# Scores of a self-attention pair as two 64-row plain fp32 products, in place of stacked and split q and k

## The reference, cut to what matters

```
DIM, HEADS, DHEAD = 160, 20, 64
q = (norm(x) @ wq1), k = (norm(x) @ wk1), v = (norm(x) @ wv1)      # 160 -> 20 heads x 64
scores = einsum('bhnd,bhmd->bhnm', q, k) * DHEAD ** -0.5           # 4 x 20 x 512 x 512
attn = softmax(scores); out = einsum('bhnm,bhmd->bhnd', attn, v)
x = out @ wo1 + bo1 + x
```

## Time and profile before

| | |
|---|---|
| median of 3 runs (lowest, highest) | 1209.48 us (1207.38, 1214.39) |
| span of the profiled execution, first to last instruction | 1209.3 us |
| mean granted TensorE clock of that execution, as a share of full | 0.983 |
| busy: TensorE / VectorE / ScalarE / GpSimd | 1143.5 / 748.8 / 621.4 / 355.7 us |
| self-attention, from its first q projection to its last output projection | 213 to 888 us of the span |
| bytes moved by the stacking DMAs' queue in all | 75.54 MB |

### The profile page before, as it was taken

The page is one execution under the profiler, slowest core; times in us unless marked ns, Lnnn a source line. Parts: engine busy times, 40 slices in busy tenths (PEclk is TensorE's granted clock), DMA queues, the critical chain, the costliest instruction groups (busy, mean ns, idle before and its releaser), DMA issues. The chain is left out here.

```text
span 1209.3 us, 21134 instructions
## 1 busy us (share of the span) xinstructions
PE 1143.5 (95%) x6348; PEld 766.6 (63%) x6348; DVE 748.8 (62%) x1758; ACT 621.4 (51%) x1370; POOL 355.7 (29%) x470
## 2 busy tenths in 40 slices
PE   7999999599999899999999999999989999999898
PEld 3555555456666666657566567666577778786787
DVE  4374574377777377774777775777637575757253
ACT  2543444356566366663565663656516464646242
POOL 2330321233433133432334332333213131312110
PEclk9999999799999999999999999999989999999899
DMA  6500000444444244444244443445120000000000
GB/s 167 114 1 1 0 1 1 104 105 105 106 105 105 56 105 106 111 99 107 58 111 107 95 108 81 111 103 118 42 55 2 1 0 0 0 1 1 1 22 22
DMA packets 43427, 76.69 MB, mean 63 GB/s; under 512 B 13316, under 2 KB 21444, under 8 KB 43332
## 3 DMA queue, kind: packets, MB, share of 16 engines
q1 hardware_dynamic: 43332, 75.54, 27.0%
HBM read 11.29 MB, written 1.31 MB: 10 GB/s over the span
## 5 line engine op out<-in xcount | busy, mean ns | idle before, releaser
L524 ACT ACTIVATE sa_probs<-banks,sa_negmax 128x512 f32<-128x512 f32 x320 | 220.9, 690 | 268.1 <-DVE sa_negmax L595 267.5
L665 POOL TENSOR_SCALAR sa_probs<-sa_probs,sa_inverse 128x512 f32<-128x512 f32 x320 | 223.1, 698 | 418.6 <-DVE sa_inverse L600 418.6
L595 DVE TENSOR_REDUCE sa_negmax<-banks 128x1 f32<-128x512 f32 x320 | 219.5, 686 | 104.8 <-PE banks L417 104.6
L427 PEld LDWEIGHTS banks<-ident,sa_probs 128*128 128x128 f32 x1280 | 146.5, 140 | 150.1 <-issue 69.1
L605 DVE COPY sa_turned<-banks 128x512 f32<-128x512 f32 x240 | 162.8, 679 | 66.4 <-PE banks L427 66.0
L427 PE MATMUL banks<-ident,sa_probs 128*128 128x128 f32 x1280 | 200.1, 279 | 1.1 <-issue 1.1
L446 PE MATMUL banks<-sa_turned,sa_v 128*64 128x512 f32 x640 | 172.6, 617 | 3.0 <-ACT sa_turned L535 1.7
L416 PE MATMUL banks<-sa_k_stack,sa_q_stack 128*128 128x512 f32 x320 | 144.8, 453 | 19.3 <-DMA sa_k_stack<-sa_k_parts 8.2
L417 PE MATMUL banks<-sa_k_stack,sa_q_stack 128*128 128x512 f32 x320 | 127.8, 399 | 0.0
L1537 POOL TENSOR_TENSOR ca_probs<-ca_probs,ca_inverse 128x616 f32<-128x616 f32 x40 | 48.8, 1219 | 162.4 <-DVE ca_inverse L1485 162.4
L416 PEld LDWEIGHTS banks<-sa_k_stack,sa_q_stack 128*128 128x128 f32 x320 | 61.3, 192 | 28.8 <-ACT sa_probs L524 13.6
(11 more groups left out here) (189 smaller groups left out, 1992.2 us busy)
## 6 DMA issues: line engine op xcount, KB each, us to landing
sa_k_stack<-sa_k_parts SPq DMA_DIRECT2D x160, 256.0 KB, 4.2
sa_q_stack<-sa_q_parts SPq DMA_DIRECT2D x160, 128.0 KB, 2.3
w_o<-in_L_xattn_wo SPq DMA_DIRECT2D x2, 800.0 KB, 6.3
out<-x SPq DMA_DIRECT2D x4, 320.0 KB, 2.5
x<-in_x SPq DMA_DIRECT2D x1, 960.0 KB, 5.3
ad_raw_main<-in_L_xattn_wq SPq DMA_DIRECT2D x1, 640.0 KB, 4.6
ad_raw_main<-in_L_xattn_wk SPq DMA_DIRECT2D x1, 640.0 KB, 7.4
ad_raw_main<-in_L_xattn_wv SPq DMA_DIRECT2D x1, 640.0 KB, 10.0
```

The source lines that it names most:

```text
L427: last = pe.transpose(b_turn[n % 2][:, q * P:(q + 1) * P], probs[:, h % PS, q, k * P:(k + 1) * P], ident[:])
L524: act.activation(probs[:, h % PS, q, :], b_scores[n % 2], ACT.Exp, bias=negmax[:, c:c + 1], accum_out=total[:, c:c + 1]).then_inc(s_exp.se ...
L595: dve.tensor_reduce(negmax[:, c:c + 1], b_scores[n % 2], AX_X, ALU.max, negate=True).then_inc(s_max.sem, 1)
L665: pool.tensor_scalar(probs[:, h % PS, q, :], probs[:, h % PS, q, :], inverse[:, c:c + 1], 1.0, ALU.mult, ALU.mult).then_inc(s_norm.sem, 1)
```

## The change

- Scores: `q_all` and `k_all` hold a pair's q and k unsplit, head 0 on partitions 0 to 63, head 1 on 64 to 127, as the projection leaves them. `scores(b, u)` multiplies both heads of the pair for one query block, one head on array rows 0 to 63 and one on rows 64 to 127, each as one plain fp32 product (L368 in the changed file), into two banks of their own.
- The rounding of q and k, the remainders and all eight DMAs per pair are gone. ScalarE copies q, VectorE copies k.
- The order of work is in units. One maximum (VectorE) of 128 x 2 x 512, two exponentials, one reciprocal, two scalings and eight transposes make up one unit. Turned tiles for head 1 are copied by ScalarE in every second unit, the others by VectorE.
- PSUM: scores take four banks instead of two; `b_out` and `b_proj` become one bank each instead of two. So projections of q, k and v each wait for the copy of the one before, and the output projection uses the turned tiles' banks.
- After every unit with `u % 4` of 0, 1 or 2, the q, k or v of pair `u // 4 + 2` is projected; after `u % 4 == 3` none is. The normalised x is turned in two halves, at units 23 and 27, into the one projection bank. Before `pv` of the last unit, the output projection's products of the first eight pairs for the first 128 rows are made (four pairs before).

**TensorE, middle of a pass, a stretch without a projection, before**: turning head 0, scores of one block (`sa_k_stack`, `sa_q_stack`), `pv` for both heads, turning head 1.

The diff, cut to its core:

```diff
-    LEAD, LAG = 10, 2
-    NB = H1 * QT
-    PAIRB = 2 * QT
+    NU = NPAIR * QT
+    LEAD = 5
...
-    LN_AT = 37
-    TURN_AT = (NPAIR - 3) * PAIRB + 1
-    PROJECT, ROUND, REST = (20, 19, 16), (19, 18, 15), (18, 17)
-    START = {1: (1, 0), 2: (1, 1), 3: (1, 2), 8: (2, 0), 9: (2, 1)}
+    RING = 8
+    LN_AT = 12
+    TURN_MAIN, TURN_TAIL, ROUND_AT = 23, 27, 31
+    START = {0: (1, 0), 1: (1, 1), 2: (1, 2)}
+    def part_at(u):
+        j, what = u // QT + 2, u % QT
+        return (j, what) if what < 3 else None
...
-        q_stack = sb("q_stack", [P, 2, 2, S], F32R)
-        k_stack = sb("k_stack", [P, 2, 2, 2, S], F32R)
-        q_parts = sb("q_parts", [P, 2, S], F32R)
-        k_parts = sb("k_parts", [P, 2, S], F32R)
+        q_all = sb("q_all", [P, 2, S])
+        k_all = sb("k_all", [P, 2, S])
...
-        b_scores, b_turn, b_out, b_proj = banks[0:2], banks[2:4], banks[4:6], banks[6:8]
+        b_scores, b_turn, b_out, b_proj = [banks.pair(0), banks.pair(2)], banks[4:6], banks[6], banks[7]
...
-                for e, rows, half, to in places:
-                    sp.dma_start(k_stack[to, s, e, :, :].bitcast(F32), k_parts[rows, :, :].bitcast(F32)).then_inc(s_stack[s].sem, 16)
...
+            def scores(b, u):
+                j, q = divmod(u, QT)
+                if q == 0:
+                    pe.wait_ge(s_ksb.sem, s_ksb.at(b, j))
+                pe.wait_ge(s_exp.sem, s_exp.at(b, 2 * u - 3))
+                bank = b_scores[u % 2]
+                for e in range(2):
+                    rows = slice(e * HD, (e + 1) * HD)
+                    last = pe.matmul(bank[:, e, :], q_all[rows, j % 2, q * P:(q + 1) * P], k_all[rows, j % 2, :], start=True, stop=True)
+                last.then_inc(s_scores.sem, 1)
...
+            def batch(b, more):
+                for u in range(NU):
+                    m = u + LEAD
+                    if m < NU:
+                        scores(b, m)
+                    elif more:
+                        scores(b + 1, m - NU)
+                    if u >= 1:
+                        pv(b, u - 1)
+                    turns(b, u)
...
+                wait_turned_copied(pe, b, NU - 1, 0)
+                pe.wait_ge(s_att.sem, s_att.at(b, NPAIR - 2))
+                project_out(0, 0, NPAIR - 2)
+                pv(b, NU - 1)
...
+            def exps(b, u):
+                j, q = divmod(u, QT)
+                act.wait_ge(s_max.sem, s_max.at(b, u))
+                if q == 0:
+                    act.wait_ge(s_turn.sem, s_turn.at(b, 2 * QT * (j - 1) - 1))
+                for e in range(2):
+                    act.activation(probs[:, j % 2, e, q, :], b_scores[u % 2][:, e, :], ACT.Exp, bias=negmax[:, u % RING, e:e + 1],
+                                   accum_out=total[:, u % RING, e:e + 1]).then_inc(s_exp.sem, 1)
...
-                dve.tensor_reduce(negmax[:, c:c + 1], b_scores[n % 2], AX_X, ALU.max, negate=True).then_inc(s_max.sem, 1)
+                dve.tensor_reduce(negmax[:, u % RING, :], b_scores[u % 2], AX_X, ALU.max, negate=True).then_inc(s_max.sem, 1)
```

More of the change, by code:

```diff
@@ L611, in update @@
                         dve.wait_ge(s_bias.sem, s_bias.at(b, 0))
[L612 to L623 removed]
+                    xt = x[:, bass.ds(b * QT + 2 * half, 2), :].rearrange("p a d -> p (a d)")
@@ L625, in batch @@
+                    dve.tensor_tensor(xt, b_turn[half][:, 0:2 * D], xt, ALU.add).then_inc(s_x.sem, 1)
+            copy_k(0, 0)
+            for u in range(LEAD):
+                maxima(0, u)
+                if u in START and START[u][1] == 1:
+                    copy_k(0, START[u][0])
+                if u >= 1:
+                    inverses(0, u - 1)
             def batch(b, more):
-                for n in range(NB):
-                    m = n + LEAD
-                    if m < NB:
+                for u in range(NU):
+                    m = u + LEAD
+                    if m < NU:
```

411 lines of the change are left out of this document (167 added, 244 removed).

## The result

The changed kernel takes 1244.23 us (median of 4 runs, 1241.88 to 1246.55), the kernel before 1208.84 us beside it. The ratio is 1.0286, with a 95% interval of 1.0237 to 1.0335: slower by 2.9%. The forecast was 1236 us with a range of 1216 to 1267. The profiled execution has a span of 1244.6 us, 35.3 more than before, and the following is read against it.

The account below looks back on a forecast made before the run. TensorE was taken as the bound, with ScalarE's chain bounding every fourth interval. Passes 1 to 3 +31.1, pass 4 +13.0, gaps -6.8, start -12.9, end -1.1, small gaps +3.4: together +26.7 on 1209.3, 1236 us, range 1216 to 1267.

Parts of the forecast that it names:

- small gaps: Between TensorE's products: summed intervals gave 14.59 where rows have 14.68, 0.022 per interval, 156 times, +3.4 us.
- gaps: Between passes: 16.5 us in gaps 1 and 2 against about 18.9, 13.7 in gap 3 against 15.6; -6.8 us.
- start: First q projection to first `pv`, without the stacking DMAs: first `pv` near 236.3 us, -12.9 us.
- Price of the pair: Two heads' plain fp32 scores on TensorE: 1.01 us against 0.94 before, range 0.86 to 1.22.
- The chain: Units with `u % 4 == 3`: `pv` waits for ScalarE's copy behind two exponentials; interval 4.14 summed, 4.10 us used, before 2.97.
- The pass's last interval: Each pass's end: two transpose runs, a bank-freeing copy and 16 output projection records ahead of the last `pv`, 4.70 us.
- The seven units at the end of pass 4: No scores beside them; `pv`, transposes and two copies with signals stand in a row, 2.9 us each.
- Hidden costs: Turning x at units 23 and 27 lies in ScalarE's wait; uncovered, 2 x 0.5 us per pass come back.
- the low end: Whole kernel with a score pair at 0.86 us, 0.15 less in some 118 projection intervals: -18, 1218 us.
- the serial rival: Scores: the two heads do not run at once, a pair costs 1.87 us, kernel 1340 us; chance 10%.
- The late ScalarE: ScalarE's order delays `pv` in two intervals of four, 0.4 us 80 times, +32, 1265 us; chance 7%.
- no faster: Rival for scores: plain products on 64 rows stream at half cost, pair 0.58 us, kernel 1186 us; chance 4%.

Follow-up runs that it names:

- the copy first: Changed kernel with ScalarE's copy of the turned tile ahead of the two exponentials in units with `u % 4 == 3`: 1215.37 us, ratio 1.0041.
- the rounded products: Changed kernel with `q_all` and `k_all` stored rounded, one rounded product per head on its 64 rows, remainders left out: 1191.94 us, ratio 0.9837.
- the run with the pair twice: Changed kernel with each unit's two score products made twice in a row, in the same banks: 1359.22 us, ratio 1.1222.
- the written-out kernels: Four passes as code in a row, not a loop: kernel before 1204.32 us, changed kernel 1246.3, split products on 64 rows with copy first 1203.19.
- the run whose start took 24.01 us at 0.86: Changed kernel with its four passes written out on TensorE, ScalarE, VectorE and GpSimd: 1246.3 us, ratio 1.0319.
- Six rounded products on 64 rows: Changed kernel with q and k split again, unstacked, three rounded products per head, and ScalarE's copy ahead of the exponentials: 1206.66 us, ratio 0.9958.

## Why the prediction was right

The sign, the mechanism and both of its halves held: plain fp32 side by side is no cheaper than four fast products, and every fourth unit waits for ScalarE. The experiments part the two: the copy first gives back about 29 us, which is ScalarE's share, and the rounded products shorten the full intervals by the 0.63 us of streaming. By the steps of the sum:

| term | forecast | measured |
|---|---|---|
| passes 1 to 3 | +31.1 (and 3.4 for small gaps in all four) | +39.3 |
| pass 4 | +13.0 | +17.6 |
| gaps | -6.8 | -8.1 |
| start | -12.9 | -10.1 |
| end | -1.1 | -1.1 |
| self-attention | +26.7 | +37.65 |
| clock ahead of and behind it | none | +2.3, -4.7 |

- *Price of the pair.* The range of 0.86 to 1.22 held, and both parts were seen: 0.86 is the streaming (the run with the pair twice), 0.20 is paid once per visit. I took 1.01 from `pv`; measured 1.06, and the 0.05 is the difference between the first records, 0.69 here and 0.64 in `pv`. An interval with a projection is 4.04 on average and not 3.96 and 0.022 of small gaps: 0.055 over 110 such intervals, 6.0 us, the largest term of the miss. By its parts: the scores 0.05 more, the projection with the hole behind it 1.11 where 0.93 and 0.08 were taken, 0.10 more; the eight transposes in one run 0.85 and not 0.92, 0.07 less, and `pv` as forecast.
- *The chain.* 4.14 summed, 4.10 used, 4.12 measured in passes 1 to 3, as forecast. In pass 4 it is 4.27, for the longer hand-overs of written-out code, which the sum did not know: 8 x 0.15, 1.2 us.
- *The pass's last interval.* 4.91, 4.82 in pass 4, against 4.70: 0.7 us in all. *The seven units at the end of pass 4*: 3.1 on average where 2.9 was taken, 1.3 us.
- *Gaps.* 15.77, 15.74 and 13.98 against 16.5, 16.5 and 13.7. The mechanism (a branch back in two of three) was shown by VectorE's pause behind its branch and by the written-out kernels, in all of which the three gaps are alike. Its size here was 1.8 us, not 2.8. The forecast took VectorE's 3.66 us from the kernel before, where the pause is 3.5 us; in the changed kernel it is 2.75.
- *Start.* 25.71 us and not 22.9. The 22.9 is itself not what its steps add up to: 6.1 to the end of v, 2.3, 7.5, 1.6 and 3.0 make 20.5. Measured, the five steps took 6.7, 3.0, 9.0, 2.4 and 4.6. Of the last, 1.5 us are clock, by the run whose start took 24.01 us at 0.86. The largest of the others is ScalarE's: its list of four units stood still for 2.5 us in waits for maxima, 1.9 of them for the third, whose scores stood behind a k projection that waited 1.10 us for the single bank.
- *Hidden costs.* The turning of x in the chain's shadow was right in place and size: 0.44 us each once the chain is gone (forecast 0.5). The interval behind unit 31, 0.46 us a pass longer once the chain is gone, I had not seen.
- *Slips in the sums.* The ends and the rivals are worked out with 118 intervals with a projection; the sum itself has 29 in each of three passes and 23 in the fourth, 110. With 110 the low end is about 1220 and not 1218, and the serial rival about 1334 and not 1340. The late ScalarE is 1236 + 32 = 1268 and not 1265, which puts it just above the range's upper end of 1267. None of this changes the forecast.
- *Outside self-attention.* I had no term for the clock. It gave 4.7 us back and took 2.3. By this luck the total looks better than the sum: a miss of 11.0 us in self-attention shows as 8.6 in the span.

The rivals: with the heads not at once an interval would be 4.9, and it is 4.03; their records start 0.007 us apart, and a pair added costs 0.86. So they run at once. The Trainium skill's "TensorEngine Tiling (Array Packing)", Tiling Modes, lists two independent tiles of 64 rows; the trace agrees. ScalarE's order did not spread: in intervals with a projection `pv` waits for nothing. Only the first ones of passes 2 and 3 are longer, 4.27 and 4.23: behind the gap the two products of `pv` start 0.25 to 0.30 us apart. And on 64 rows a plain product streams at 0.86 a pair, what the records of `pv` gave for 128 rows, and no faster.

What stays open: why the first record of a pair lasts 0.10 us longer than the second. It could be the load of 128 columns or the change of shape; no run told them apart. For the load speaks that the first records of the scores are 0.05 us longer than those of `pv`, and so are the loads, 0.186 against 0.133. In the run with the pair twice, the second pair's loads last as long and its first records are not longer.

## What to carry to other kernels

Price a change of operands on the engine that bounds: two plain fp32 products side by side (0.86 us, 1.06 with what is paid once per visit) cost as much as four rounded ones of full height (0.23 each) or more. So unsplit operands save the other engines' work and none of the bound's. When blocks are joined to larger units, write down for each in-order engine what now stands in one lump ahead of the operation that the bounding engine waits for: moving one copy ahead of two exponentials gave back 29 of the 35 us. And before a version is called faster, give the old kernel the same side edits: written-out passes alone were worth 0.6% there.

## What the runs showed of the hardware

- One more change of the array's shape per unit costs 0.19 us. A visit to half-height products costs 0.20 us once, and 0.86 for each pair of plain fp32 products streamed.
- Six rounded products on 64 rows, two at once, take 0.88 us, less than two plain fp32 ones on the same rows (1.06).
- In the run of the rounded products the clock fell to 1.2 GHz for part of an interval in 7 of 36 intervals behind a chain's, in which TensorE had been idle for 1.6 to 1.7 us (granted 0.66; 3.40 became 4.97), and not in the other 29, most of them with the same wait. In the changed kernel, whose chain waits were 0.95 us, 1.11 in pass 4, it never fell inside a pass. And whole stretches at the low level come and go outside the changed code: 4.4 us for identical work.
- The same chain of hand-overs takes 0.15 us longer in code written out than in the loop, while each branch back costs 1.8 to 3.3 us: VectorE's next instruction comes 2.7 to 3.5 us behind it.
